# First half of the skip term's addition placed in front of the first stage's normalisation on VectorE

## The reference, cut to what matters

```python
x = x + _L0_gnn_ref(_layernorm(x), adj, L0_gnn_W, L0_gnn_a)
x = x + _L0_ffn_ref(_layernorm(x), L0_ffn_W_in, ...)         # the Mamba-2 block
x = x + _L1_gnn_ref(_layernorm(x), L1_gnn_adj, adj, L1_gnn_weight, L1_gnn_bias)
x = x + _L1_ffn_ref(_layernorm(x), L1_ffn_gate_w, ...)       # the experts
```

```python
Y = (Y_diag + Y_off + xh * D[:, None]).reshape(Bsz, L, D_INNER)
Y = Y * jax.nn.silu(z)
Y = Y * jax.lax.rsqrt(jnp.mean(Y * Y, axis=-1, keepdims=True) + EPS) * norm_w
out = Y @ W_out
return out @ W_lin + b_lin
```

## Time and profile before

| | |
|---|---|
| time, median of 3 runs | 3693.07 us (3690.87 to 3696.62) |
| time of the profiled execution | 3692.86 us |
| its span, first to last instruction | 3691.1 us |
| TensorE busy | 3452.6 us (94%) |
| TensorE weight loads busy | 2780.1 us (75%) |
| VectorE busy | 2537.9 us (69%) |
| GpSimd busy | 1807.0 us (49%) |
| ScalarE busy | 1743.9 us (47%) |
| granted TensorE clock, mean | 0.985 of full speed |

### The profile page before, as it was taken

The page is one execution under the profiler, slowest core; times in us unless marked ns, Lnnn a source line. Parts: engine busy times, 40 slices in busy tenths (PEclk is TensorE's granted clock), DMA queues, the critical chain, the costliest instruction groups (busy, mean ns, idle before and its releaser), DMA issues.

```text
span 3691.1 us, 63266 instructions
## 1 busy us (share of the span) xinstructions
PE 3452.6 (94%) x19340; PEld 2780.1 (75%) x19340; DVE 2537.9 (69%) x7375; ACT 1743.9 (47%) x3691; POOL 1807.0 (49%) x2010
## 2 busy tenths in 40 slices
PE   7999999999999999999999999999699999999998
PEld 6777777777777777777777777767488888888887
DVE  4877878787787878878778778787444444444444
ACT  3555555565565555556555555555223232323232
POOL 2455545445455454554545455454345454545453
PEclk8999999999999999999999999999799999999999
DMA  3111211111121111111112121111155555555553
GB/s 118 38 39 46 36 36 40 43 37 41 42 37 38 40 40 37 46 37 37 40 37 42 35 49 35 36 40 33 51 191 198 193 197 193 196 194 195 195 194 129
DMA packets 168177, 304.60 MB, mean 83 GB/s; under 512 B 38016, under 2 KB 140416, under 8 KB 149952
## 3 DMA queue, kind: packets, MB, share of 16 engines
q0 software_dynamic: 38272, 196.98, 15.4%
q1 hardware_dynamic: 92896, 72.41, 6.4%
q10 hardware_dynamic: 36960, 34.62, 6.2%
HBM read 250.77 MB, written 53.17 MB: 82 GB/s over the span
## 4 chain that ended last, share of the span: by engine, by line
PE 53%; DVE 25%; POOL 12%; issue 9%; ACT 1%; DVEq 0%; DMA 0%; ACTq 0%; POOLq 0%; SPq 0%
PE bank L1398 13%; PE bank L1412 13%; PE bank L1133 7%; POOL masks L482 6%; DVE conv L827 6%; PE bank L1149 5%; PE bank L1237 4%; PE bank L1350 4%; DVE y L1009 3%; POOL row L468 2%; DVE y L1014 2%; POOL rstd L468 2%; DVE stats L808 2%; DVE xn L818 1%; PE bank L1268 1%
## 5 line engine op out<-in xcount | busy, mean ns | idle before, releaser
L748 ACT ACTIVATE decay<-bank,w_up 128x256 f32<-128x256 f32 x568 | 268.8, 473 | 699.9 <-PE bank L1398 699.9
L1133 PE MATMUL bank<-xn1T,w_in 128*128 128x256 f32 x2304 | 524.9, 381 | 11.2 <-issue 9.4
L1149 PE MATMUL bank<-w_rel,hT 128*128 128x264 f32 x2048 | 506.7, 391 | 0.0
L1398 PE MATMUL bank<-zs,w_up 128*128 128x256 f32 x2272 | 503.5, 380 | 0.6 <-ACT zs L607 0.6
L1412 PE MATMUL bank<-w_dn,decay 128*128 128x256 f32 x2272 | 502.1, 379 | 0.0
L1133 PEld LDWEIGHTS bank<-xn1T,w_in 128*128 128x128 f32 x2304 | 431.6, 190 | 71.9 <-issue 12.0
L827 DVE SCALAR_TENSOR_TENSOR conv<-bank,conv_w,conv 128x255 f32<-128x255 f32 (+2 forms) x960 | 461.2, 480 | 34.8
L1398 PEld LDWEIGHTS bank<-zs,w_up 128*128 128x128 f32 x2272 | 432.7, 190 | 60.0 <-issue 0.9
L1412 PEld LDWEIGHTS bank<-w_dn,decay 128*128 128x128 f32 x2272 | 426.2, 190 | 55.1
L1081 DVE TENSOR_TENSOR hT<-bank,w_dn 128x256 f32<-128x256 f32 x142 | 60.3, 425 | 535.9 <-PE bank L1412 535.9
L1149 PEld LDWEIGHTS bank<-w_rel,hT 128*128 128x128 f32 x2048 | 369.2, 190 | 73.3 <-ACT hT L607 13.0
(11 more groups left out here) (238 smaller groups left out, 6189.7 us busy)
## 6 DMA issues: line engine op xcount, KB each, us to landing
token_rows<-row SPq DMA_DIRECT2D x64, 266.0 KB, 2.8
xT_sb<-in_xT ACTq DMA_DIRECT2D x64, 256.0 KB
x_sb<-in_x ACTq DMA_DIRECT2D x64, 256.0 KB, 2.7
adj_sb<-in_adj SPq DMA_DIRECT2D x64, 256.0 KB, 3.0
adjt_sb<-in_adjT SPq DMA_DIRECT2D x64, 256.0 KB, 3.0
out<-row SPq DMA_DIRECT2D x64, 256.0 KB, 2.2
w_in<-token_rows,idc POOLq DMA_INDIRECT x142, 4.7
out<-hT,ids POOLq DMA_INDIRECT x142, 2.4
```

The lines of the kernel that those rows point to most:

```text
L748: nc.scalar.activation(hid(f), bank[f % 4][:, 0:GROUP], ACT.Relu, bias=b1[q % 2][:, f:f + 1]).then_inc(hid_ready, 1)
L1133: ins = mm(dst, w_in[:, k, first:first + P], xn1T[:, k, :], start=k == 0, stop=k == DK - 1)
L1149: ins = mm(bank[6 + t][:, 0:GX], hT[:, d, r * N + t * P:r * N + (t + 1) * P], w_rel[:, r, d, :], start=r == 0 and d == 0, stop=r == R - 1 ...
L1398: ins = mm(bank[f % 4][:, 0:GROUP], w1[i][:, k, f * P:(f + 1) * P], xgT[:, k, :], start=k == 0, stop=k == DK - 1)
```

## The change

The loop over the two halves of y is now outside, and `normalise` of xn1 stands within it, in the first half, between the skip additions and the wait for `yd_ready`. The order on VectorE was: waits for xn1_turned and rstd_ready, xn1, wait for y_made, first half's additions, wait for yd_ready, first half's product, second half. It is now: wait for y_made (and out_made), first half's additions, waits for xn1_turned and rstd_ready, xn1, wait for yd_ready, first half's product, second half. The instructions and the semaphores are the same, and the other engines' lists are untouched.

```diff
-                if b1_ is not None:
-                    need(dve, xn1_turned, b1_)
-                    normalise(1, xn1, x1, xn1_ready, b1_)
-                if b2_ is not None:
-                    for u in range(2):
+                for u in range(2):
+                    if b2_ is not None:
                         dve.wait_ge(y_made, 2 * b2_ + 1 + u)
                         if u == 0:
                             need(dve, out_made, b2_)
...
                                                          bank[2 + u][:, (j % 2) * N:(j % 2 + 1) * N], ALU.mult,
                                                          ALU.add)
                         ins.then_inc(yd_ready, 1)
+                    if b1_ is not None and u == 0:
+                        need(dve, xn1_turned, b1_)
+                        normalise(1, xn1, x1, xn1_ready, b1_)
+                    if b2_ is not None:
                         dve.wait_ge(yd_ready, 2 * b2_ + 1 + u)
                         v.tensor_tensor(y[:, 2 * u:2 * u + 2, :], y[:, 2 * u:2 * u + 2, :], zs[:, 2 * u:2 * u + 2, :],
                                         ALU.mult).then_inc(yz_ready, 1)
```

## The result

| | before | changed |
|---|---|---|
| time, median of 5 runs each | 3690.95 us (3686.05 to 3696.62) | 3625.66 us (3622.0 to 3628.05) |
| profiled execution | 3692.86 us | 3625.17 us |
| span | 3691.1 us | 3623.4 us |
| granted TensorE clock, mean | 0.985 | 0.989 |
| VectorE idle before xn | 46.3 us | 2.6 us |

The ratio is 0.9822, 95% interval 0.9808 to 0.9835: faster by 65.3 us. I had forecast 3639 us with a range of 3633 to 3667. The direction and the place are right; the gain is 12 to 14 us larger than forecast, and the time lies under the range.

A forecast was written before the change was run, and what follows sets the result against it. Neither TensorE nor VectorE was full; the chain of handovers bound the kernel, passing VectorE's wait before xn. 63 steps at 0.85 us give 53.6 us: 3692.86 - 53.6 = 3639.3, so 3639 us, range 3633 to 3667.

The forecast's parts named there:

- The wait is on the chain, in each of 63 steps: VectorE's idle time before xn at a step's end, 0.69 us, was claimed to lie on the chain in 63 steps.
- The input is there and xn loses nothing: L1333's matmuls end 1.46 us before VectorE is free, so the moved y_made wait holds up nothing; xn starts 0.02 us later.
- 0.85 us a step: Likeliest earlier start of both gate products on VectorE, repeated in 63 steps: 53.6 us; chance 0.79.
- the upper bound of 0.88: Most a step could gain: 0.69 idle filled, 0.08 overlap with router instructions, 0.11 from the separated dependent pair.
- the dependent pair: First product waiting for the additions right in front of it on VectorE; putting xn between was to save 0.11 us.
- The 0.77: Gain per step if, by the skill's rule, the dependent pair's last 0.11 us did not count: 3644.4 us.
- What is late next: After the change TensorE still waits by 0.2 us; ScalarE's square stays covered by 0.1 us; later work moves earlier as a whole.
- The power beside the additions: Rival: additions slow GpSimd's power for rstd; xn late, gain 11 us (3682), or half in milder form (3666); chance 0.07.
- The addition did not wait for the power: Rival: VectorE's additions wait for GpSimd's power through the same ports; gain 13 us, 3680 us; chance 0.03.
- y_made was never late: Rival: late y_made blocks in-order VectorE, xn behind it; loss up to 0.54 us a step, 3727 us; chance 0.03.
- no other engine took over: Rival: ScalarE or TensorE cover too small, or a load holds the next step; half the gain lost, 3666 us; chance 0.05.
- a granted clock of 1.00: Read from the 2490.4 us window of 62 steps, from the first skip addition to the last step's normalisation.

The follow-up runs named there:

- experiment 2: Changed kernel plus unread VectorE work (two additions and a tiny one) between normalisation and first product, so products start as late as before: 3679.66 us, ratio 0.9968.
- experiment 6: Kernel before with only the first of the two additions moved in front of the wait for rstd, the second left behind xn: 3662.31 us, ratio 0.9929.
- experiment 1: Kernel before plus eight unread TensorE turns, four before its wait for xn and four behind xn's turn, and a wait for x3_ready: 3683.95 us, ratio 0.998.
- experiment 4: Changed kernel plus three unread additions and a tiny one (about 1.3 us) between normalisation and first product: 3735.69 us, ratio 1.0125.
- experiment 8's second kernel: Kernel before plus one unread 512-element addition, one source in SBUF and one in PSUM, in front of the wait for rstd: 3689.29 us.
- experiment 8: Kernel before plus one unread 512-element addition before the wait for rstd: both sources in SBUF 3697.77 us, one in PSUM 3689.29 us.

## Why the prediction was wrong, point by point

- **The wait is on the chain, in each of 63 steps**: right. All 63 distances shrank, their medians by 0.91 and 0.92 us; experiments 2 and 6 took the gain back and halved it.
- **The input is there and xn loses nothing**: right. No idle time stands in front of the additions, and xn starts 0.70 us behind the router instructions (0.69 before).
- **0.85 us a step**: a little small, and so was the upper bound of 0.88. My own spacings gave 0.88; the 0.03 I took off for a late semaphore wait do not exist, the dependent pair costs 0.12 rather than 0.11, and the spans between are 0.02 shorter. With the 57.7 us of the distances the sum is 3692.9 - 57.7 = 3635 us, still inside the range. The 0.77 that I had worked out from the Trainium skill ("VectorE: DVE Perf Modes", section "The DRAIN you can't avoid") would have been further off.
- **What is late next**: right. TensorE's turn, ScalarE's squares and the queues behind them kept their place.
- **The step that failed is a missing term.** I read a granted clock of 1.00 for the middle part and costed everything at it, so the sum has nothing for the clock. That number is rounded: seven short stretches at the lower clock lie in the window, and six of them stand behind the very waits of TensorE that the change shortens. The changed kernel has none there until its last step with both graphs, where both kernels have one. In the profiled pair this is worth 6.0 us, and it alone takes the sum under the range: 3692.9 - 57.7 - 6.0 = 3629 us. That the clock follows those waits is shown by experiment 1 (waits filled, VectorE as before: 6.3 us faster) and experiment 4 (waits longer: 27 stretches). Experiment 2 went against it as I had first put it: with waits only 0.05 us shorter than before the stretches were gone. Why the kernel before has them in some pairs and not in others I can't say.
- **The last 4 us** down to 3625.2 lie outside the 63 distances: 2.7 us before the first second product, of which the mechanism explains 0.9, and 1.3 behind the last. Their cause is open, and they need not be the change's: experiment 8's second kernel has the steps of before and yet only 81.2 us to its first second product. Without them the time would still have been under the range.
- **The rivals**: none took place. The power beside the additions kept its median of 0.709 us; experiment 8 bears out both the danger and the reason given against it. The addition did not wait for the power, y_made was never late, and no other engine took over.

## What to carry to other kernels

A wait on the chain is worth the independent work that fits into it and no more, and an independent instruction put between a dependent pair saves a little beside; before moving work into a wait, look what that work covered where it stood. An estimate made at full clock leaves out what TensorE's idle time does to the clock: sum the waits at the place of the change, and look in narrow windows whether the clock falls behind them, since a mean of 1.00 can hide it.

## What the runs showed of the hardware

- TensorE's granted clock fell to 1.2 GHz for 3.4 us at a time at the end of a step, where no single wait was longer than 1.19 us: 27 times in some 28 pairs of steps with waits of 0.79, 1.19 and 0.35 us, 5 and 8 times with 0.79, 0.85 and 0.35, and not once with 0.79, 0.80 and 0.35 or with 1.57 and 0.35. Extra matmuls in those waits, 8 turns a step, made the kernel 6.3 us faster.
- GpSimd's power of 128x2 elements took 1.36 us instead of 0.77 in 12 of 63 steps beside a VectorE addition with both sources in SBUF, which itself kept its 0.68 us, and never beside one with a source in PSUM.
- A VectorE instruction that needs the one right in front of it started 0.03 us behind that one's end; where it did not need it, it started 0.08 us before the end. An independent instruction put between a dependent pair made a step 0.12 us shorter.
